# A Mamba scan's skip term and dead-state product moved between VectorE, ScalarE and GpSimd, with the step projection's input in two halves

## The reference

```python
xz = jnp.einsum('bld,ed->ble', x, Win)
u, z = jnp.split(xz, 2, axis=-1)
uc = _silu(conv(u))                                # 4 taps along the sequence
x_dbl = jnp.einsum('bld,ed->ble', uc, Wx)          # 16 step inputs, B and C of 32 states each
dt = jax.nn.softplus(jnp.einsum('blr,dr->bld', x_dbl[..., :16], Wdt) + bdt)
# per step: h = exp(dt*A)*h + (dt*u)*B ; y = sum over states of h*C
y = ys + uc * Dp
y = y * _silu(z)
return jnp.einsum('bld,ed->ble', y, Wout)
```

## Time and profile before

| | us |
|---|---|
| median of 3 timed runs | 4176.53 |
| lowest and highest | 4160.9, 4176.98 |
| the profiled execution: time | 4170.99 |
| its span, first to last instruction | 4169.4 |

### The profile page before, as it was taken

The page is one execution under the profiler, slowest core; times in us unless marked ns, Lnnn a source line. Parts: engine busy times, 40 slices in busy tenths (PEclk is TensorE's granted clock), DMA queues, the critical chain, the costliest instruction groups (busy, mean ns, idle before and its releaser), DMA issues. The chain is left out here.

```text
span 4169.4 us, 69953 instructions
## 1 busy us (share of the span) xinstructions
PE 3876.4 (93%) x19212; PEld 2887.9 (69%) x19213; DVE 3632.0 (87%) x6958; ACT 2802.3 (67%) x4602; POOL 2351.2 (56%) x1949
## 2 busy tenths in 40 slices
PE   6999999999999999999999968888888699999998
PEld 4666666666666666666666646776777588888887
DVE  7999999999999999999999948888888566666665
ACT  5777777777777777777777746666667244454444
POOL 2555555455565545555554556776667555565555
PEclk8889888888898888889888889999999699999999
DMA  2222122122221222222122222222222455555555
GB/s 71 46 48 48 43 40 54 44 50 48 47 45 40 54 44 52 47 49 44 39 53 44 47 50 97 83 86 80 84 84 81 133 96 85 95 105 94 87 94 86
DMA packets 198463, 272.59 MB, mean 65 GB/s; under 512 B 23377, under 2 KB 143058, under 8 KB 198354
## 3 DMA queue, kind: packets, MB, share of 16 engines
q0 software_dynamic: 94432, 130.60, 17.9%
q1 hardware_dynamic: 100480, 138.48, 12.1%
q10 hardware_dynamic: 3442, 2.21, 0.2%
HBM read 121.07 MB, written 150.14 MB: 65 GB/s over the span
## 5 line engine op out<-in xcount | busy, mean ns | idle before, releaser
L618 PE MATMUL pj<-xt,win 128*128 128x512 f32 x3144 | 937.3, 458 | 49.1 <-DVE xt L793 28.4
L618 PEld LDWEIGHTS pj<-xt,win 128*128 128x128 f32 x3144 | 685.7, 222 | 276.5 <-issue 53.5
L2016 POOL DMA_INDIRECT out<-e_y,e_to x272 | 472.3, 1736 | 365.8 <-ACT e_y L2122 306.1
L806 DVE SCALAR_TENSOR_TENSOR uc<-pj,convw,uc 128x511 f32<-128x511 f32 (+2 forms) x780 | 516.8, 728 | 4.6 <-ACT uc L411 4.6
L326 POOL TENSOR_TENSOR wk<-v,uc 128x512 f32<-128x512 f32 x260 | 347.4, 1336 | 280.9 <-DVE v L854 280.2
L666 PE MATMUL po<-yz,wout 128*128 128x512 f32 x1024 | 456.6, 599 | 0.0
L301 POOL TENSOR_TENSOR r<-r,neg_half 128x4 f32<-128x4 f32 x64 | 77.7, 1214 | 666.2 <-ACT r L387 666.2
L2067 PE MATMUL e_p<-e_w,e_a 128*128 128x256 f32 x3264 | 415.8, 284 | 0.8 <-DVE e_a L2177 0.8
L2067 PEld LDWEIGHTS e_p<-e_w,e_a 128*128 128x128 f32 x3264 | 393.4, 188 | 11.0 <-DVE e_a L2177 2.2
L2055 PE MATMUL e_p<-e_xt,e_w 128*128 128x512 f32 x1632 | 395.1, 397 | 4.1 <-DVE e_xt L2169 2.4
L666 PEld LDWEIGHTS po<-yz,wout 128*128 128x128 f32 x1024 | 189.3, 190 | 262.8 <-issue 262.8
(11 more groups left out here) (244 smaller groups left out, 8849.5 us busy)
## 6 DMA issues: line engine op xcount, KB each, us to landing
e_x<-expert_in SPq DMA_DIRECT2D x138, 260.0 KB, 2.6
bb<-bc SPq DMA_DIRECT2D x65, 512.0 KB, 6.0
h_rows<-fb POOLq DMA_DIRECT2D x64, 512.0 KB, 7.1
h_rows<-h0c SPq DMA_DIRECT2D x32, 512.0 KB, 6.3
a_h<-h_rows SPq DMA_DIRECT2D x128, 128.0 KB
out<-a_bs SPq DMA_DIRECT2D x128, 128.0 KB
bc<-xd SPq DMA_DIRECT2D x65, 128.0 KB, 2.3
e_w1s<-in_moe_w POOLq DMA_DIRECT2D x9, 512.0 KB, 5.6
```

The source lines that it names most:

```text
L618: i = mm(pj[m][:], win[d][wp][:, k, c:c + P], xt[xp][:, k, :], start=(k == 0 and n == 0), stop=(k == KD - 1 and n == 2))
L806: stt(uc[d][:, m, to], pj[m][:, of], convw[d][:, m, tap:tap + 1], uc[d][:, m, to], ALU.mult, ALU.add).then_inc(S["cv"], 1)
L2016: pool.indirect_dma_start(out=out, out_offset=bass.IndirectOffsetOnAxis(ap=to[n][:, j:j + 1].bitcast(U32), axis=0), in_=y[n][:, j, :], in_ ...
```

## The change

The skip term is no longer made by VectorE. ScalarE scales `uc` in place by `dp` (`skip`, four operations a turn, two behind the decays, two in the next `front` between the silu halves), once GpSimd has read `uc` for the scan input. The dead states' product reads GpSimd's `wk` (= dt*u) in place of `v`, and GpSimd adds the scaled `uc` to it (`add_input`, two adds of two tiles), at the head of its slot. GpSimd now makes all four `wk` ahead of the four `tp`, and waits for the broadcast only before the latter; `keep_residual` moves from the forward to the backward turn. On TensorE `x_dbl` runs in two halves, each behind one half of z, and the order behind it is row squares, step projection, fusion. On ScalarE z's four silus stand together, and the table load comes ahead of `xd_copy`. VectorE's `ln_stats` moves behind `dead_part`. Waits follow the new writers and readers. The core of the diff:

```diff
                 dst = h1_dram[bass.ds(s * SEQ, SEQ), :].rearrange("(j p) c -> p j c", p=P)
                 pool.dma_start(dst, fb[d][:], accum_op=ALU.add).then_inc(S["acc"], 16)
-            def scan_inputs(t, d, tiles=range(MD)):
+            def scan_inputs(t, d):
+                pool.wait_ge(S["dt_ok"], t + 1)
+                for m in range(MD):
+                    pool.tensor_tensor(wk[:, m, :], v[:, m, :], uc[d][:, m, :], ALU.mult).then_inc(S["dtu_ok"], 1)
                 pool.wait_ge(S["bcast"], 16 * (t + 1))
-                for m in tiles:
-                    pool.wait_ge(S["dt_ok"], t + 1)
-                    pool.tensor_tensor(wk[:, m, :], v[:, m, :], uc[d][:, m, :], ALU.mult).then_inc(S["dtu_ok"], 1)
+                for m in range(MD):
                     pool.wait_ge(S["dtu_ok"], MD * t + m + 1)
                     if not (isinstance(t, int) and t == 0):
                         pool.wait_ge(S["yz_ok"], NP * (t - 1) + m // 2 + 1)
                     pool.tensor_tensor(tp[:, m, :], wk[:, m, :], bb[d][:, 0, :], ALU.mult).then_inc(S["tp_ok"], 1)
+            def add_input(t, d):
+                for h in range(NP):
+                    mm = slice(2 * h, 2 * h + 2)
+                    pool.wait_ge(S["q_ok"], NP * t + h + 1)
+                    pool.wait_ge(S["du_ok"], MD * t + 2 * h + 2)
+                    pool.tensor_tensor(qq[:, mm, :], qq[:, mm, :], uc[d][:, mm, :], ALU.add).then_inc(S["q2_ok"], 1)
             gather(0)
             ln_scale(0)
...
             def slots(s, first):
                 for d in range(DIRS):
                     t = 2 * s + d
+                    add_input(t, d)
                     if d == 0:
                         ln_scale(s + 1)
+                    else:
+                        keep_residual(s + 1)
                     if not first:
                         add_rows(t - 2, d, s - 1)
                     if not (first and d == 0):
                         row_scale(t - 1)
                     if d == 0:
-                        scan_inputs(t + 1, 1, range(2))
-                        keep_residual(s + 1)
-                        scan_inputs(t + 1, 1, range(2, MD))
+                        scan_inputs(t + 1, 1)
                     else:
                         pool.wait_ge(S["gt_ok"], 2 * t + 4)
                         gather(s + 2)
...
                 for m in tiles:
                     act.wait_ge(S["dt_ps"], MD * t + m + 1)
                     if not (isinstance(t, int) and t == 0):
-                        act.wait_ge(S["q_ok"], NP * (t - 1) + m // 2 + 1)
                         act.wait_ge(S["dtu_ok"], MD * (t - 1) + m + 1)
                         act.wait_ge(S["da_ok"], MD * (t - 1) + m + 1)
                     act.activation(v[:, m, :], pj[m][:], ACT.Identity, bias=bdt[d][:, m:m + 1]
...
                     act.wait_ge(S["y_ok"], NP * t + h + 1)
                     if not (isinstance(t, int) and t == 0):
                         act.wait_ge(S["tp_ok"], MD * (t - 1) + 2 * h + 2)
+                        act.wait_ge(S["q_ok"], NP * (t - 1) + h + 1)
                     act.activation(wk[:, mm, :], y[:, mm, :], ACT.Identity, bias=1.0).then_inc(S["w_ok"], 1)
             def softplus_log(t, halves=range(NP)):
...
                 for m in range(MD):
                     act.wait_ge(S["dt_ok"], t + 1)
                     act.activation(y[:, m, :], v[:, m, :], ACT.Exp, scale=amat[d][:, m, 0:1]).then_inc(S["da_ok"], 1)
+            def skip(t, d, tiles):
+                for m in tiles:
+                    act.wait_ge(S["dtu_ok"], MD * t + m + 1)
+                    act.activation(uc[d][:, m, :], uc[d][:, m, :], ACT.Copy, scale=dp[d][:, m:m + 1]
+                                   ).then_inc(S["du_ok"], 1)
             def project_copies(t):
...
             def front(t, d, s_next=None):
                 uc_silu(t, d, range(2))
-                z_silu(t, d, range(2))
+                if not (isinstance(t, int) and t == 0):
+                    skip(t - 1, 1 - d, range(2, MD))
                 uc_silu(t, d, range(2, MD))
+                z_silu(t, d, range(MD))
+                act.preload_act_table_set("natural_log_exp_and_others")
                 xd_copy(t, d)
-                z_silu(t, d, range(2, MD))
                 if s_next is not None:
                     ln_apply(s_next)
-                act.preload_act_table_set("natural_log_exp_and_others")
             def back(t, d, copies):
...
                 if copies:
                     project_copies(t - 1)
                 decays(t, d)
+                skip(t, d, range(2))
                 act.preload_act_table_set("silu_and_others")
             act.wait_ge(S["c_tab"], 2)
...
                                    start=(k == 0 and n == 0), stop=(k == KD - 1 and n == 2))
                     i.then_inc(S[ps], 1)
-            def x_dbl(t, d):
+            def x_dbl(t, d, tiles):
                 if not (isinstance(t, int) and t == 0):
                     pe.wait_ge(S["fl_ok"], 3 * t)
-                for m in range(MD):
+                for m in tiles:
                     pe.wait_ge(S["uc_ok"], MD * t + m + 1)
                     i = mm(px[0:NXR, :], wx[d][:, m, :], uc[d][:, m, :], start=(m == 0), stop=(m == MD - 1))
-                i.then_inc(S["xd_ps"], 1)
+                if MD - 1 in tiles:
+                    i.then_inc(S["xd_ps"], 1)
             def dt_proj(t, d):
                 pe.wait_ge(S["xd_ok"], t + 1)
...
             def front(t, d, s_next, turn, back):
                 in_proj(t, d, 1, range(2))
+                x_dbl(t, d, range(2))
+                in_proj(t, d, 1, range(2, MD))
+                x_dbl(t, d, range(2, MD))
+                if back > 1:
+                    row_squares(t - 2)
+                dt_proj(t, d)
                 if back > 1:
                     fusion(t - 2, d)
-                x_dbl(t, d)
-                in_proj(t, d, 1, range(2, MD))
-                dt_proj(t, d)
-                if back > 1:
-                    row_squares(t - 2)
                 if turn:
                     turn_x(s_next)
                 if isinstance(t, int) and t == 0:
...
                 dve.wait_ge(S["s_ps"], t + 1)
                 dve.wait_ge(S["fl_ok"], 3 * t + 2)
                 for h, mm in pairs():
-                    stt(qq[:, mm, :], over_pair(pss[:]), dall[:], v[:, mm, :], ALU.mult, ALU.mult
+                    dve.wait_ge(S["dtu_ok"], MD * t + 2 * h + 2)
+                    stt(qq[:, mm, :], over_pair(pss[:]), dall[:], wk[:, mm, :], ALU.mult, ALU.mult
                         ).then_inc(S["q_ok"], 1)
-                for m in range(MD):
-                    dve.wait_ge(S["q_ok"], NP * t + m // 2 + 1)
-                    stt(qq[:, m, :], qq[:, m, :], dp[d][:, m:m + 1], uc[d][:, m, :], ALU.add, ALU.mult
-                        ).then_inc(S["q2_ok"], 1)
             def outputs(t, d):
                 dve.wait_ge(S["h_ok"], MD * (t + 1))
...
                 for h, mm in pairs():
                     dve.wait_ge(S["hc_ok"], t + 1)
-                    dve.wait_ge(S["q2_ok"], MD * t + 2 * h + 2)
+                    dve.wait_ge(S["q2_ok"], NP * t + h + 1)
                     tt(tp[:, mm, :], tp[:, mm, :], qq[:, mm, :], ALU.add).then_inc(S["yv_ok"], 1)
             def gate(t, d):
...
                 for d in range(DIRS):
                     t = 2 * s + d
                     conv(t + 1, 1 - d)
+                    dead_part(t, d)
                     if d == 0:
                         ln_stats(s + 1)
-                    dead_part(t, d)
                     scan(t, d)
                     bc_product(t + 1, 1 - d)
                     outputs(t, d)
```

More of the change, by code:

```diff
@@ L145, in mamba_stage @@
           u_ps a_ok z_ps z_ok uc_ok xd_ps xd_ok bc_ok bcast xd_st dt_ps v_ok vc_ok y_ok l_ok w_ok g_ok
-          d0_ok dt_ok dtu_ok tp_ok da_ok h_ok hc_ok q_ok q2_ok yv_ok yz_ok xm_ok qd_ps gt_ok ct_ok cnt_ps
+          d0_ok dt_ok dtu_ok tp_ok da_ok h_ok hc_ok q_ok du_ok q2_ok yv_ok yz_ok xm_ok qd_ps gt_ok ct_ok cnt_ps
           fl_ok s_ps o_ps fo_ok sq_ok ss_ps rv_ok rr_ok f_ps fin_ok h1_st acc gt2 e_bc e_da e_tp e_h e_hc e_y""".split()
@@ L408, in last_tap_and_bias @@
                     if not (isinstance(t, int) and t < 2):
-                        act.wait_ge(S["q2_ok"], MD * (t - 2) + m + 1)
+                        act.wait_ge(S["q2_ok"], NP * (t - 2) + m // 2 + 1)
                         act.wait_ge(S["dtu_ok"], MD * (t - 2) + m + 1)
@@ L903, in more_states @@
                             dve.wait_ge(S["e_hc"], at)
-                            dve.wait_ge(S["q2_ok"], MD * (t + 1))
+                            dve.wait_ge(S["q2_ok"], NP * (t + 1))
                             tt(qq[:, m, :], qq[:, m, :], eh, ALU.add).then_inc(S["e_y"], 1)
```

## The result

The changed kernel takes 4448.84 us (median of 4 runs, 4439.91 to 4454.26) beside 4171.48 for the kernel before on the same chip: a ratio of 1.0666, 95% interval 1.0635 to 1.0697. It is slower, as forecast, but by 277 us in place of 177; the time lies above the stated range, which ended at 4410. The profiled execution took 4454.26 us, its span 4452.4.

The account below looks back on a forecast made before the run. VectorE bound the kernel, TensorE close behind; after the change TensorE's turns, 37.64 backward and 40.71 forward, make a pair of 78.35 against 72.82 us: 5.53 × 32 = 177, 4171 + 177 = 4348 us, range 4188 to 4410.

Parts of the forecast that it names:

- What bounds the kernel: Scan stage: VectorE (99% busy) sets the pace, TensorE (97%) close behind; relieving one gains only what the other can spare.
- TensorE's gap: TensorE between out projection and `x_dbl`: 6.8 us, about 3 idle, waiting for ScalarE's first silu behind two scalings.
- The clock term: TensorE's falls from 2.4 to 1.2 GHz: taken to cost 3.8 us a pair of turns, as before the change.
- today's cost: Clock loss in the kernel before, seen in u: 1.2 + 2.6 = 3.8 us a pair, kept for the forecast.
- twice the falls, 82: Upper bound of TensorE's pair of turns, 82 us, if the clock falls twice as often.
- Rival 1: Full clock on TensorE: fusion keeps it up, new gap too short; pair 74.6, 4228 us; full or half, chance 0.18.
- u takes about 6 us in every turn: TensorE's u group: a sign that would show the forecast wrong.
- The backward turn: TensorE's sum from out projection to out projection in a backward turn: 37.64 us.
- The forward path over GpSimd: GpSimd's adds ahead of the layer-norm scale delay the low part of x; this path alone makes forward turns 40.7 us.
- rival 2: GpSimd's adds beside VectorE's scans: adds take 6.6 for 4.8 us, scans lose 2.2, hidden; 4405 us, chance 0.12.
- ScalarE's scalings: Four on ScalarE, 2.56 us a turn, borne as a sum; two add 1.28 to TensorE's gap, the others nothing.
- Rival 3: Faster: ScalarE's stretch to the first silu keeps TensorE's gap below about 5.9 us at full clock; 4145 us, chance 0.10.

Follow-up runs that it names:

- The run without adds and scalings: Changed kernel with the fusion back behind z's first half, without GpSimd's two adds and ScalarE's four scalings a turn: 4161.00 us, 0.9975.
- the filled gap: Changed kernel with z's first half computed twice on TensorE, in its idle time ahead of `x_dbl`: 4331.46 us, 1.0385.
- the last experiment: Kernel before, with GpSimd's four `wk` ahead of the four `tp` and the residual's add held until the slot's scans are done: 4135.28 us, 0.9909.

## Why the prediction was right or wrong

The loss by its causes, in stage ends (after, less each edit in turn): fusion's place 2672.8 − 2545.8 = 127.0; adds 2545.8 − 2433.9 = 111.9; scalings 2433.9 − 2358.8 = 75.1; the relief itself 2358.8 − 2393.5 = −34.7. Together 279.3. The shares hold for this order of taking away, and for single executions; the adds alone were worth 30 us while the fusion stood, and behind the scale they cost next to nothing (2437.4 beside 2433.9).

**What bounds the kernel** was right: two engines nearly full, relief worth what TensorE has to spare. The run without adds and scalings shows it: 34.7 us, with TensorE at 98.6%.

**TensorE's gap** was right: from the projection's end to `x_dbl` 6.8 forecast and 6.88 in the rows (1139.15 − 1132.27), "about 3 us" of it idle, released by ScalarE's silu; 4.13 and 3.22 in the rows, 214.2 in all.

**The clock term** is the step that failed. The sum took "today's cost", 3.8 us a pair, all of it in u. In the pair of the rows above u lost nothing; from start to start and against the same groups of the turn with the filled gap, the first half of `x_dbl` lost 1.42 and 1.41, z's second half 0.97 and 1.46, the step projection 0.51 and 0.04, the fusion against its 3.45 before 2.93 and 1.79: 10.5 us. 78.35 − 3.8 + 10.5 = 85.1, against 83.7 in this pair and 81.64 in the mean.

Nor was today's cost all in u: the sum took the dead sums at 1.79 in each turn and the turning of x at 1.69, from rows at the lower clock, and they now take 0.98 (1201.60 − 1200.62) and 0.96 (1159.29 − 1158.33), which brings 85.1 to 82.7.

The bound "twice the falls, 82" held the measured mean; the forecast named two stretches in which the clock could fall and counted the cost of one fall a turn, and the range was then cut at 4410, short of that bound (72.82 to 82 is 294 us: 4465).

The falls rose from 64 to 111 in 64 turns, and they moved to work that others wait for: u's slowness had cost TensorE's time, the fusion's delays x. The kernel's own turns agree: the 6 forward turns whose first fall comes 6.4 to 7.2 us behind the step's end, over z's first half, take 40.4 us, and the 25 where it comes 12.5 to 14.4 us behind, around `x_dbl` after the gap, 41.7 to 46.2, most of them over 44. They don't prove it, since `x_dbl` also starts earlier in the six, 10.4 us behind the step's end in place of 13.1 to 14.6.

With the gap filled the kernel takes 4331, 17 from the forecast, and the pair 77.85 beside 78.35. Of that the forward turn, held by GpSimd's path, was forecast as such; the backward one, held by VectorE, is near by luck.

The Trainium skill's "TensorE: Matmul & The Clock Gate", section "HAM oscillation — how this bites in real kernels", says that idle gaps between bursts of products, if they last long enough, bring the lower clock back. The filled gap bears it out (granted clock 0.88 to 0.95), though the gap of 3.2 us brought a fall only in some turns. The prediction read from it that the cost would stay, not that the gap's fall would come on top.

**Rival 1** fails: the fusion doesn't keep the clock up, it runs at half speed for most of its 6.54 us in the rows.

**"u takes about 6 us in every turn"** stood in the list of what would show the forecast wrong on the fast side. It came true in a slower kernel. A fall that leaves one group has to be looked for in the others before it counts as gone.

**The backward turn**: 37.64 forecast, 37.61 measured, but by luck: the forecast is TensorE's sum. In the backward turn of the rows VectorE waits 0.27 us in 37.5, while TensorE stands for 3.86 (3.22 and 0.64): the scans' loss used up the spare that the prediction gave VectorE. Without the adds, with the fusion in its new place, it is 36.10.

**The forward path over GpSimd** was right: 40.7, with the low part of x 29.6 us behind the step's end. With the falls mostly gone, the kernel with the filled gap shows 40.60 and 1182.44 − 1153.08 = 29.36; with the fusion back it is 40.44, and with the scale ahead of the adds in addition 37.06. In the changed kernel it is for the most part hidden behind the slower TensorE. The two rows with the filled gap:

```profile
1153.08 2.27 DVE L876 SCALAR_TENSOR_TENSOR v<-v,wk 128x2048 f32<-128x2048 f32 x1
...
1182.44 1.29 DVE L815 TENSOR_TENSOR xt<-pj,xt 128x512 fp32r<-128x512 f32 x2 [2.13 <-ACT xt L411]
```

**Contention (rival 2)**: the right mechanism with the payer and the price wrong. The adds went from 2.40 to 2.58 us, 1.08 times in place of 1.38; the scans paid 346.2 / 64 = 5.4 us a turn in place of 2.2. "A scan reads more slowly than L874" was no protection. The residual's add, whose move was put at nothing, stands beside the scans now and costs them 2.1 us in each backward turn, as the run without the other adds shows. Two single scans of a backward turn, from two narrow windows of VectorE's timeline:

```profile
1183.18 3.22 DVE L882 TENSOR_TENSOR_SCAN tp<-y,tp 128x512 f32<-128x512 f32 x1
...
1192.82 1.19 DVE L882 TENSOR_TENSOR_SCAN tp<-y,tp 128x512 f32<-128x512 f32 x1
```

GpSimd's timeline of the same stretch, the two adds and the residual's:

```profile
1182.97 5.60 POOL L339 TENSOR_TENSOR qq<-qq,uc 128x1024 f32<-128x1024 f32 x2
1188.53 3.28 POOL L308 TENSOR_TENSOR h0c<-g,cvec 128x1024 f32 x1
```

The scan that starts 0.21 us into an add takes 3.22: the rest of an undisturbed add (2.35 in the last experiment's row), 2.35 − 0.21, and then its own 1.19, is 3.33. It doesn't run slower, it stands still, as L825 did above. Taking over L874's loss (4.88 against 2.73) was wrong: what counts is how long GpSimd's instruction still runs, not how fast the VectorE one reads. The Trainium skill's "SBUF — State Buffer", section "Who interferes with whom", has the rule that whichever starts first gets the shared ports for its whole instruction and the other blocks until it ends; these rows agree. Priced from rows in the same way, at 2.35 us for each add and two and a half adds a turn with the residual's, the scans' loss would have been 5.9 in place of 2.2 (an estimate; measured 5.4).

**ScalarE's scalings** were put in the gap rightly (1.28, measured 1.32 for two), but called 2.56 us that "ScalarE as a sum bears". Once fusion and adds are out of the way they hold the pair at 74.09 in place of 71.73.

**Rival 3** fails at its condition: the gap is 6.88 us, not under 5.9, and the clock isn't at its upper level.

## What to carry to other kernels

Before a group of products is moved out of a stretch where TensorE would otherwise wait, ask what the clock will be there and behind it, and who waits for what will run slow; a filler of useless products tells in one run whether idle time is the cause. Work given from VectorE to GpSimd may be no relief when VectorE has operations with two SBUF inputs at the same time (here 260.7 us went and 346.2 came): price each GpSimd instruction at its whole length on VectorE, or place it beside VectorE's reads of PSUM or of a single tensor. Ask too what stands behind it in GpSimd's own queue: with the fusion back, that order alone was worth 108 us here. And when a slow stretch moves, follow who hangs on it, not only its length.

## What the runs showed of the hardware

A VectorE operation of 128x4 took 2.17 us in place of 0.16 because GpSimd's add of 128x1024 had begun 0.36 us earlier; a scan beside one such add took 3.22 and beside two in a row 5.77 (1138.76, the first of four that took 9.12 together; its record starts 0.04 us ahead of the adds, and it stood still even so) in place of 1.19. And 3 us of useless products a turn made a kernel 117 us faster: the granted clock of the stretch was 0.95 in place of 0.88. Not settled: why one gap of 3.2 us ahead of `x_dbl` brings a fall of the clock and the next doesn't; and what the scans' standing still costs by itself, since with the fusion back and the scale first the backward turn is 0.77 us longer than in the run without adds and the forward one 0.62 shorter.
